# Softmax denominators of cross attention: nine steps of ones matmuls a head group, or joins of partial sums by DMA and two steps

## The reference, cut to what matters

```
q = split_heads(layernorm(x) @ Wq.T + bq)        # 16 heads x 512 x 32
k = split_heads(ctx @ Wk.T + bk)                 # 16 heads x 8192 x 32
v = split_heads(ctx @ Wv.T + bv)
attn = softmax(q k^T * 32 ** -0.5, axis=-1)
x = x + (attn v) @ Wo.T + bo
```

## Time and profile before

| | us |
|---|---|
| median of 3 runs | 1579.67 (1578.26 to 1581.8) |
| span of the profiled execution | 1576.5 |
| cross attention in it, from the first to the last weighted sum | 577.8 to 1135.9 |

### The profile page before, as it was taken

How to read it: one execution, slowest core, us unless ns; L and a number is a source line. 1 busy time by engine, 2 the same in 40 slices (tenths; PEclk the granted TensorE clock), 3 DMA queues, 4 the chain that set the end, 5 groups by cost and what they waited for, 6 DMA issues and landing times. The chain is left out here.

```text
span 1576.5 us, 23638 instructions
## 1 busy us (share of the span) xinstructions
PE 1508.9 (96%) x8658; PEld 869.0 (55%) x8658; DVE 1240.5 (79%) x1876; ACT 1021.3 (65%) x1343; POOL 411.2 (26%) x225
## 2 busy tenths in 40 slices
PE   6899999999999999999999999999999965999998
PEld 4566666666666554444443444444445732799995
DVE  6877676776767869999998999999876878476664
ACT  3466666666666768888888888888726941244441
POOL 5564545636447010502100400100004420100002
PEclk9999999999999999999999999999999987899999
DMA  6354444444444455456646444545247045399994
GB/s 234 131 189 141 174 174 142 179 153 167 165 157 160 126 142 129 120 129 189 158 114 153 114 127 114 127 114 128 61 54 161 2 159 223 127 340 349 360 333 140
DMA packets 119777, 254.57 MB, mean 161 GB/s; under 512 B 10152, under 2 KB 26536, under 8 KB 115184
## 3 DMA queue, kind: packets, MB, share of 16 engines
q1 hardware_dynamic: 117632, 248.35, 51.1%
q0 software_dynamic: 1408, 4.46, 0.9%
q10 hardware_dynamic: 624, 0.27, 0.1%
HBM read 182.26 MB, written 61.34 MB: 155 GB/s over the span
## 5 line engine op out<-in xcount | busy, mean ns | idle before, releaser
L800 ACT ACTIVATE att_pr<-b_sc 128x1024 f32<-128x1024 f32 x512 | 479.9, 1037 | 82.9 <-PE b_sc L700 82.2
L850 DVE TENSOR_TENSOR att_tot<-att_tot,att_pr 128x2048 f32<-128x2048 f32 x184 | 427.3, 2322 | 21.6 <-ACT att_pr L800 3.4
L519 DVE CUSTOM_DVE_ANT_0 ctx_size<-ctx_tot,ctx_size 128x512 f32<-128x512 f32 x512 | 333.0, 688 | 127.2 <-PE ctx_tot L430 124.1
L481 ACT ACTIVATE ctx_size<-ctx_dif 128x1024 f32<-128x1024 f32 x256 | 262.5, 1025 | 120.0 <-PE ctx_dif L430 120.0
L700 PE MATMUL b_sc<-g_stacks,att_kst 98*128 98x512 f32 x1024 | 298.5, 422 | 1.9 <-DMA att_kst<-keys_scratch 1.7
L700 PEld LDWEIGHTS b_sc<-g_stacks,att_kst 98*128 98x128 f32 x1024 | 174.7, 189 | 192.2 <-ACT att_pr L800 143.2
L714 PE MATMUL b_o<-att_pr,att_val 128*32 128x512 f32 x2048 | 258.4, 602 | 0.9 <-issue 0.9
L430 PE MATMUL ctx_dif<-ctx_k_dif,f_q_hi 32*128 32x512 f32 x512 | 128.2, 497 | 5.8 <-DVE ctx_best L519 4.5
L430 PE MATMUL ctx_tot<-ctx_k_sum,f_q_hi 32*128 32x512 f32 x512 | 127.8, 497 | 0.0
L86 PE MATMUL f_proj<-f_wv_hi,g_stacks 128*128 128x512 f32 x320 | 120.5, 420 | 0.0
L86 PE MATMUL f_proj<-g_stacks,f_wk_hi 128*128 128x512 f32 x352 | 119.4, 420 | 0.3 <-DVE f_k_lo L211 0.3
(11 more groups left out here) (314 smaller groups left out, 2177.2 us busy)
## 6 DMA issues: line engine op xcount, KB each, us to landing
m_w<-in_W SPq DMA_DIRECT2D x30, 2048.0 KB, 10.1
att_kst<-keys_scratch SPq DMA_DIRECT2D x192, 256.0 KB, 4.0
f_raw<-in_ctx SPq DMA_DIRECT2D x32, 1024.0 KB, 6.0
keys_scratch<-f_k_hi SPq DMA_DIRECT2D x32, 512.0 KB, 2.8
keys_scratch<-f_k_lo SPq DMA_DIRECT2D x32, 512.0 KB, 3.2
values_scratch<-ctx_v SPq DMA_DIRECT2D x32, 512.0 KB, 3.4
att_val<-values_scratch SPq DMA_DIRECT2D x64, 256.0 KB, 2.7
rows_scratch<-mix_blank SPq DMA_DIRECT2D x1, 3840.0 KB, 24.1
```

Of the source, the lines that this page charges most:

```text
L481: act.activation(size[:, i % ABS, :], dif[:, :], ACT.Abs).then_inc(s_size, 1)
L519: dve.tensor_tensor_reduce(out=size[:, i % ABS, r * CH:(r + 1) * CH], in0=tot[i % 2][:, r * CH:(r + 1) * CH], in1=size[:, i % ABS, r * CH: ...
L800: act.activation(pr[:, T % SLOTS, 2 * s:2 * s + 2, :], sc[(2 * T + s) % PAIRS][:, :].rearrange("p (j q) -> p j q", j=2), ACT.Exp, scale=SC ...
L850: dve.tensor_tensor(tot[b % 2][:, :, :], so_far, pr[:, T % SLOTS, :, :], ALU.add).then_inc(s_add, 1)
```

## The change

Runs are five units long (twelve of five and one of four a group, thirteen runs). Runs 0 to 11 of a group are joined: after a run's last add, GpSimd issues a transfer that adds the run's `tot` onto that of the group's run 0 (`base`), from SBUF to SBUF, 1 MiB, with `accum_op` and at most 2048 bytes to a descriptor; 11 such joins a group, each waiting for the one before. The partial sums now have three rooms (`c.hT`, not in use during this stage, is the third). TensorE does two steps of sums a group: one on the joined tile, one on run 12's. They stand behind a weighted sum of the next group (u = 5, 4 and 6 for the first three groups; at the end for the last). VectorE's first add of a run waits for the join of the run that had the room before, or for the steps of sums of the last group. The inversion moves to u = 8, the turn to u = 13, and GpSimd's order is: join 1, weigh, join 2, rows, joins 3 to 11, and in group 0 the output bias behind them.

```diff
--- before.py
+++ after.py
@@ -553,10 +553,24 @@
     TILES = G * PER_G
     SLOTS = 6
     PAIRS = 3
-    RUNS = (8, 7, 7, 7, 7, 7, 7, 7, 7)
-    TURN = 9
+    RUNS = (5,) * 12 + (4,)
+    JOINED = len(RUNS) - 2
+    TURN = 13
     LAG = 4
+    INVERT = 8
     starts = [g * PER_G + sum(RUNS[:b]) for g in range(G) for b in range(len(RUNS))]
+    base = [0]
+    for _ in range(G - 1):
+        base.append([n for n in range(3) if n != base[-1]][(len(RUNS) - 1) % 2])
+
+    def room(b):
+
+        g, k = divmod(b, len(RUNS))
+        return base[g] if k == 0 else [n for n in range(3) if n != base[g]][(k - 1) % 2]
+
+    def joins(g, k):
+
+        return 16 * (g * JOINED + k)
 
     def run_of(T):
 
@@ -572,7 +586,7 @@
         kst = [sb(f"kst{b}", [STK + 2, HG, CH], F32R) for b in range(CHUNKS)]
         val = [sb(f"val{b}", [P, KT, P]) for b in range(CHUNKS)]
         pr = sb("pr", [P, SLOTS, HG, N])
-        tot = [sb(f"tot{b}", [P, HG, N]) for b in range(2)]
+        tot = [sb(f"tot{b}", [P, HG, N]) for b in range(2)] + [c.hT]
         rs = sb("rs", [P, N])
         whole = sb("whole", [P, N])
         sc, o, den = c.sc, c.o, c.den
@@ -580,7 +594,7 @@
         v_in = [sem(f"v_in{b}") for b in range(CHUNKS)]
         s_ones, s_sc, s_exp, s_pv, s_add, s_sum, s_whole = (
             sem(n) for n in ("ones", "sc", "exp", "pv", "add", "sum", "whole"))
-        s_rs, s_norm, s_out = sem("rs"), sem("norm"), sem("out")
+        s_rs, s_norm, s_out, s_join = sem("rs"), sem("norm"), sem("out"), sem("join")
         s_row = [sem(f"row{half}") for half in range(2)]
         shift_hi = sb("shift_hi", [P, H, NT], F32R)
         stats = sb("stats", [P, NT, 6])
@@ -630,20 +644,35 @@
             for b in range(1, CHUNKS):
                 pool.memset(f32(kst[b][MROW:MROW + 2, :, :]), 1.0).then_inc(s_ones, 1)
             pool.wait_ge(s_ones, CHUNKS)
-            pool.wait_ge(bo_in, 16)
-            for t in range(NT):
-                pool.tensor_tensor(c.x[:, t, :], c.x[:, t, :], c.yT[:, 2, :], ALU.add).then_inc(s_bo, 1)
-            pool.wait_ge(s_bo, NT)
-            for g in range(G - 1):
+            def join(g, k):
+
+                b = g * len(RUNS) + k
+                pool.wait_ge(s_add, adds(starts[b] + RUNS[k] - 1))
+                if g or k > 1:
+                    pool.wait_ge(s_join, joins(g, k - 1))
+                pool.dma_start(tot[base[g]][:, :, :], tot[room(b)][:, :, :], accum_op=ALU.add,
+                               max_dma_last_dim=4 * N).then_inc(s_join, 16)
+
+            for g in range(G):
+                join(g, 1)
                 if g:
+                    pool.wait_ge(s_rs, g)
+                    pool.wait_ge(s_whole, g)
+                    weigh(pool, g - 1)
                     pool.wait_ge(s_out, g)
-                pool.wait_ge(s_stage, g + 1)
-                for h in range(HG * (g + 1), HG * (g + 2)):
-                    take_row(pool, h, stage, s_row[0])
-                    pool.wait_ge(s_row[0], HG // 2 + h - HG + 1)
-                pool.wait_ge(s_rs, g + 1)
-                pool.wait_ge(s_whole, g + 1)
-                weigh(pool, g)
+                join(g, 2)
+                if g + 1 < G:
+                    pool.wait_ge(s_stage, g + 1)
+                    for h in range(HG * (g + 1), HG * (g + 2)):
+                        take_row(pool, h, stage, s_row[0])
+                        pool.wait_ge(s_row[0], HG // 2 + h - HG + 1)
+                for k in range(3, JOINED + 1):
+                    join(g, k)
+                if g == 0:
+                    pool.wait_ge(bo_in, 16)
+                    for t in range(NT):
+                        pool.tensor_tensor(c.x[:, t, :], c.x[:, t, :], c.yT[:, 2, :], ALU.add).then_inc(s_bo, 1)
+                    pool.wait_ge(s_bo, NT)
 
         @block.sync
         def _(sp):
@@ -715,22 +744,24 @@
                                    start=first, stop=False, skip_group_check=True)
                 mm.then_inc(s_pv, 1)
 
-            def sums(b):
-
-
-                last = (starts + [TILES])[b + 1] - 1
-                g, first = b // len(RUNS), b % len(RUNS) == 0
-                if first and g:
+            def sums(g):
+
+                b = len(RUNS) * (g + 1) - 1
+                if g:
 
                     pe.wait_ge(s_rs, g)
-                if first and g + 1 < G:
+                if g + 1 < G:
                     pe.wait_ge(s_stage, g + 1)
-                pe.wait_ge(s_add, adds(last))
-                for j in range(HG):
-                    mm = pe.matmul(den[HD * j:HD * j + HD, :], c.ones[:, :], tot[b % 2][:, j, :],
-                                   start=first, stop=False, skip_group_check=True)
+                pe.wait_ge(s_join, joins(g, JOINED))
+                for n, tile in enumerate((tot[base[g]], tot[room(b)])):
+                    if n:
+                        pe.wait_ge(s_add, adds(PER_G * (g + 1) - 1))
+                    for j in range(HG):
+                        mm = pe.matmul(den[HD * j:HD * j + HD, :], c.ones[:, :], tile[:, j, :],
+                                       start=(n == 0), stop=False, skip_group_check=True)
                 mm.then_inc(s_sum, 1)
 
+            summed = [min(T for T in range(PER_G * g + LAG, TILES) if T % 3 == 0) for g in range(1, G)]
             for pair in range(PAIRS):
                 scores(pair)
             T = 0
@@ -739,8 +770,8 @@
                     scores(pair)
                 while T < TILES and 2 * T + 2 <= ahead:
                     weighted(T)
-                    if T - LAG in starts[1:]:
-                        sums(run_of(T) - 1)
+                    if T in summed:
+                        sums(summed.index(T))
                     g, u = divmod(T, PER_G)
                     if u == TURN and g + 1 < G:
                         if g:
@@ -758,7 +789,7 @@
             pe.wait_ge(c.wo_in, 16)
             pe.wait_ge(s_out, G - 1)
             residual(0, range(G - 1))
-            sums(len(starts) - 1)
+            sums(G - 1)
             for t in range(1, NT):
                 residual(t, range(G - 1))
             pe.wait_ge(s_out, G)
@@ -839,19 +870,26 @@
                 if v == 0:
                     return
                 dve.wait_ge(s_exp, 2 * T + 2)
+                g, k = divmod(b, len(RUNS))
                 if v == 1:
-                    if b >= 2:
-
-                        dve.wait_ge(s_sum, b - 1)
+                    if k == 0 and g:
+
+                        dve.wait_ge(s_join, joins(g, 0))
+                    elif k in (1, 2) and g:
+
+                        dve.wait_ge(s_sum, g)
+                    elif k >= 3:
+
+                        dve.wait_ge(s_join, joins(g, k - 2))
                     so_far = pr[:, (T - 1) % SLOTS, :, :]
                 else:
                     dve.wait_ge(s_add, adds(T) - 1)
-                    so_far = tot[b % 2][:, :, :]
-                dve.tensor_tensor(tot[b % 2][:, :, :], so_far, pr[:, T % SLOTS, :, :], ALU.add).then_inc(s_add, 1)
+                    so_far = tot[room(b)][:, :, :]
+                dve.tensor_tensor(tot[room(b)][:, :, :], so_far, pr[:, T % SLOTS, :, :], ALU.add).then_inc(s_add, 1)
 
             def invert(g):
 
-                dve.wait_ge(s_sum, len(RUNS) * (g + 1))
+                dve.wait_ge(s_sum, g + 1)
                 if g:
                     dve.wait_ge(s_norm, g)
                 dve.reciprocal(rs[:, :], den[:, :]).then_inc(s_rs, 1)
@@ -867,7 +905,7 @@
                         if g:
                             dve.wait_ge(s_row[0], HG // 2 + HG * g)
                         dve.tensor_copy(stage, den[:, :]).then_inc(s_stage, 1)
-                if u == LAG + 2 and g:
+                if u == INVERT and g:
                     invert(g - 1)
                 if u == PER_G - 1:
                     dve.wait_ge(s_pv, T + 1)
```

## The result

The changed kernel takes 1617.61 us (median of 4 runs, 1612.23 to 1621.34), the kernel before 1580.37 in the same comparison; the ratio is 1.0238, 95% interval 1.0219 to 1.0257: slower by 2.4%, where 1.6% less was forecast. It is the first rival, close to its milder case (1623 us).

A forecast was written before the change was run, and what follows sets the result against it. TensorE was taken to bound cross attention; 29 dropped steps of sums save 24.9 us, the end adds 0.1, so 1579.7 - 24.8 = 1554.9 us. The likeliest case lies in 1551 to 1560, the range reaches up to 1645.

The forecast's parts named there:

- first rival: Cross attention: the chain of joins becomes the bound, leading from 10.2 us a join, slower than before from 10.7; chance 0.40.
- milder case: The first rival with joins of 11.7 us each: a stage of 605 us and a time of 1623 us.
- The sum of TensorE: Cross attention: 29 dropped steps of sums at 0.86 us save 24.9, the end adds 0.1; 24.8 us less.
- L: Time of one join, from GpSimd's wait to the semaphore; taken as 9.1 us between bounds of 5.3 and 22.9.
- the edge at 10.2: The L in us at which the joins' chain equals TensorE's new stage of 537 us; the forecast lay 1.1 under.
- the upper end: Highest bound on L: a copy within SBUF doubled for adding, doubled again for key and value loads, 22.9 us.
- The chain's arithmetic: If joins lead, a group lasts 11 L plus 22.4 us, and the cross attention stage 90 + 44 L.
- the cushion: Six slots between VectorE's adds and the exponentials let VectorE be 9 us late before ScalarE stops.
- VectorE's wait for both steps: Last group: the first add of a second run waits some 2.7 us for both steps of sums, hidden.
- Rival 2: Joins slow VectorE's adds, 1.1 us for every issue: a group of 138.2 us, 1571 us in all; chance 0.06.
- Rival 3: Key loads come late through the joins' traffic, needing four times their 4.0 us; given no chance of its own.
- The signs of being wrong: Adds at a run's beginning waiting for joins, ScalarE waiting for adds, TensorE under 95%, groups of 22.4 + 11 L.

The follow-up runs named there:

- e1: The changed kernel without the 44 joins and every wait for them, sums of runs 1 to 11 left out of the denominators: 1558.94 us, ratio 0.987 to before.
- e2: The changed kernel with each key load from the fourth chunk on cut to a quarter of one row block, joins kept: 1558.55 us, ratio 0.987 to before.
- e3: The changed kernel with 8192 bytes to a descriptor in place of 2048 in the joins: 1599.51 us, ratio 1.0127 to before.
- e5: The changed kernel with joins as plain copies that overwrite the destination in place of adding: 1557.39 us, ratio 0.985 to before.

## Why the prediction was wrong

- **The sum of TensorE** (24.8 us) was right in its mechanism: without transfers, a group lasts 134.3 us to a tenth. e1 shows 22.1 us of it between the first weighted sum and the last, and 20.5 us as a time.
- **The step that failed is the value taken for L**: 9.1 us, measured 11.6 in a busy chain. Its terms were 3.3 fixed, 0.6 for GpSimd's issue and 5.2 of stream. In e2 a join of 6.3 us stream landed in 8.8 at the median (9.1 in mean), its issue included, and where the next issue waited for it, it began 0.5 us after the landing: L = 9.3 to 9.6. So the stream was 1.1 us longer than taken (5.2 was twice a load from DRAM at the 404 GB/s of the earlier trace rows; it is 6.1 to 6.3), the rest about 0.9 shorter (3.0 for 3.9), and by itself that stays under the edge at 10.2, as e2's time says too.
- **What I left out** was the 0.50 share of the loads: I had counted it for the upper end and for rival 1, and not in the value taken, since the load I took as nearest had stood beside key loads. It did so once for 2.6 us; with the engines 0.93 busy over the stage, a stream of 6 us is seldom alone. Of the 2.5 us between 9.1 and 11.6, the company cost 1.7 (mean landings, 10.8 against 9.1; at the medians, 10.1 against 8.8, it is 1.4) and the join by itself 0.5; the seven joins above were 0.3 slower than the mean of all 44.
- **The chain's arithmetic held, to some 10 us.** 90 + 44 x 11.6 = 600 us for the stage; from 580.6 to the end of the sums (1184.8) it was 604. That is 38 over 562, or 1618 us by the median of before; measured 1617.6. That it fits so closely is in part luck, since 11.6 is the first group's: with the 11.4 of all four the sum is 592. The 12 us between lie for the most part between groups (36.3, 34.9 and 39.1 us from the last join's issue to the next one, where 11.4 + 22.4 = 33.8 was reckoned). The sum gives e3 the right sign as well: its joins 3 to 11 follow one another every 11.0 us, over the 10.7 from which the change loses, though they land in 9.8 at the median; 90 + 44 x 11.0 = 574 us, measured 582, and the kernel lost 20 us.
- **Part of the cushion wasn't there.** I let VectorE be 9 us late through the six slots. At a group's end it has next to no room to be late, since the copy to `whole` stands behind its adds and the PSUM tile is single. And a stall has a second price that I had not counted: the growth of 39.2 us (32.2 + 7.0) and the 22.1 us that e1 shows as saved make 61.3, of which TensorE's waits are 46.0 (46.9, less 0.9 before). Most of the other 15 is matmuls at the 1.2 GHz level. In the trace the stage has eight stretches at a granted clock of 0.50, each at a wait of TensorE or just behind one (the shortest of 1.49 us), and summed over them TensorE is busy for 35.2 us:

```profile
sum 47.60, PE 35.20 PEld 10.44 DVE 35.74 ACT 17.97 POOL 5.17; mean PE 4.40 PEld 1.30 DVE 4.47 ACT 2.25 POOL 0.65
```

At that level two units of weighted sums last 3.56 us in place of 1.92, so by estimate 35.2 us hold 16 us that the higher level would not have cost; the kernel before paid 2 us of the kind at the stage's start (4.8 us at that level). So the trace accounts for 14 of the 15; no run takes this price away by itself.

- **VectorE's wait for both steps** was 6.59 us in the last group, not 2.7, since TensorE itself stood behind a stall.
- **Rival 2 did not occur.** 204 adds took 475.2 us, 2.33 each, against 514.8 / 220 = 2.34 before. By the Trainium skill, SBUF — State Buffer, "SBUF: two separate sides", only VectorE's two-port modes hold descriptor writing off, and an add of two tiles is not in one; the trace agrees. **Rival 3** neither: key loads landed in 6.5 us in place of 4.0, and TensorE waited for none.
- The chance of 0.40 for the rival was fair for a margin of 1.1 us on a term with ends at 5.3 and 22.9; the forecast took the low half on one load that had run beside the key loads for 2.6 us.
- **The signs of being wrong came as written:** VectorE's first adds of runs waited 67.6 us for joins (31.6 + 36.0), TensorE's share of the stage is 92%, and the groups, from copy to copy of the weighted sums, last 157.3, 148.4 and 150.5 us against 22.4 + 11 x 11.6 = 150.0.

## What to carry to other kernels

Price a transfer on busy DMA engines at its own stream (here 1.7 to 1.9 times a copy's for an addition) plus what the loads of others cost it, and compare the mean from one issue to the next, not the median landing, with the interval at which the work for it comes. In a serial chain a term that is put at 90% of that interval is no margin. Here one more unit in each run (six in place of five) bought most of what was lost, 46 us, and long descriptors the rest, 14. Look for single buffers handed over at a stage's joints: slack in a ring of slots does not reach across them. When a stall falls on TensorE, add the slow matmuls behind it to its price.

## What the runs showed of the hardware

- A 1 MiB transfer within SBUF held the 16 engines for 3.2 us as a copy (4096-byte packets, e5), for 6.1 us as an addition with 2048-byte packets and 5.3 us with 8192-byte ones (e3). Beside the key loads these landed in 6.3, 10.1 and 9.8 us (medians, issue included); the addition with 2048-byte packets landed in 8.8 where key loads were small (e2).
- GpSimd's issue took 1.29 us for an addition of 512 packets, 0.87 for one of 128, and 0.76 for the copy of 256. From a landing to the issue that waited for it, it took 0.5 us.
- Beside the joins a key load landed in 6.5 us in place of 4.0.
- TensorE's granted clock was 0.50 (1.2 GHz) around the end of a stall of 7.59 us; over the stage TensorE was busy for 35.2 us at that level, always beside a wait.
